# A gated delta rule whose keys keep their length and whose next body's matrices are made inside the solve

## The chip, the cores and the metric
The kernel runs on one core of a Trainium2 chip. The metric is the device time of one execution in microseconds (us), as the median of several runs. TensorE multiplies matrices, VectorE and ScalarE work on elements, GpSimd does the same more slowly and only in SBUF, and SyncE issues the DMAs. PSUM has eight banks of 512 fp32 columns.

## The reference
The program is one decoder layer: a layer norm, a gated delta rule (`L0_attn`), a cross attention, and a feed-forward with block quantisation. The change lies in the delta rule. Of it the reference computes, for 8 sequences of 256 tokens, 8 key heads and 16 value heads of width 128:

```
q, k, v = split(silu(causal_conv(x @ W_qkv)));  z = x @ W_z
q = l2norm(q) * DK**-0.5;  k = l2norm(k)         # x * rsqrt(sum(x*x) + 1e-6)
for t: S = S * exp(g_t);  v_adj = (v_t - k_t S) * beta_t
       S = S + k_t v_adj^T;  o_t = q_t S
o = o * rsqrt(mean(o*o) + 1e-6) * norm_weight * silu(z)
```

## The kernel before, in words
`delta_rule` runs 32 bodies that project and a 33rd that only finishes. A body takes one pair of sequences and one key head with its two value heads. The two sequences are the sets s = 0 and 1, so every buffer of `two(...)` exists twice. Each sequence is cut in two halves of 128 tokens (k = 0, 1); with the two value heads e this makes four blocks hb.

Body n solves the delta rule on q, k and v that body n - 1 projected, and projects q, k, v and z for body n + 1. The projection has six tiles of 128 channels, each of four parts of three matmuls of 512 columns (`project`, L600 to L602), 24 parts in all. The parts are dealt by hand between the steps of the solve. Two PSUM banks `proj` take them in turn. Before, the same two banks also take the decay sums, the outputs turned to channels, the sums of squares and the spread norms.

The solve goes so. `scores` makes key-key products (L622, L623) and key-query products (L628, L629). VectorE masks the key products (L1016), multiplies them by the decay and by beta to the matrix A (L1022), adds the identity to its diagonal half blocks in fp16 (L1029) and makes the first inverse (L1033). TensorE turns it (`first_inverse`, L649). Six levels then double the size of the inverted blocks: `level_r` (L665, or L661 at the last level), a mask by VectorE (L1059), `level_x` (L685 and L690, or L679), and copies by ScalarE to `inv` (L883) and `inv_t` (L887). With the inverse, each half of the tokens is solved once (`solve`, L701), its residual is taken with I + A (`residual`, L712, L1080) and a correction is added (`correct`, L719, L1086). `outputs` (L733) multiplies by the attention matrix, and `between` (L725, L726) carries the first half to the second: L1112 subtracts it from the second values, ScalarE copies them (L920) and scales the other product to `o_off` (L923). The second half is solved in the same way.

Before, keys are scaled to length one: q and k are squared (L914), `sums_of_squares` adds them (L741), VectorE adds epsilon (L1107), GpSimd takes the power -0.5 (L1195) and makes two diagonals (L1199, L1204), TensorE spreads them over the partitions (`spread_norms`, L748), and VectorE multiplies (`k_unit`, L1122). The query's norm is applied to the outputs: `next_gate` makes `q_scale` (L1008, L1011) and copies the gates (L1006).

The short convolution is three taps per tile on VectorE (`tap`, L957) behind two copies by ScalarE (`tile_copy`, L826 and L829). GpSimd also multiplies the mask by the decays (`mask_gates`, L1177), adds the identity to A (L1184), normalises the outputs (L1162 to L1170) and makes two of the steps of silu(z) (L1207, L1189). `gated` (L996) multiplies the outputs by it, and SyncE stores them (`store`, L560). Each fourth body splits the weights of the next key head into a high part (ScalarE, L838) and a low part (VectorE, L971), from tiles that SyncE loads (L555).

Each engine works through its own queue strictly as it is written in `step` of its block. What holds an instruction is a semaphore (`wait_ge`), and everything behind it on the engine waits too.

## Time and profile before

| | |
|---|---|
| median of 3 runs | 2535.69 us (2531.49 to 2535.79) |
| the profiled execution | 2537.05 us |
| its span, first to last instruction | 2535.3 us |
| TensorE / VectorE / ScalarE / GpSimd busy in the span | 2138.2 / 1936.7 / 1439.7 / 1190.9 us |
| projection lines L600, L601, L602 | 378.5 / 319.8 / 314.9 us busy, 768 matmuls each |
| taps, L957 | 388.9 us busy, 384 instructions |

"Busy" is the union of an engine's instructions. In a timeline, rows of one line that follow each other are merged (x2, x4), "idle before" is the engine's gap and what ended it, and an instruction's length can hold its wait for a port. Busy TensorE is overlapped work: what the next matmul adds is read from one start to the next.

### The profile page before, as it was taken

The page shows a single profiled execution, that of the slowest core. Times are in us where ns is not written, and L with a number is a line of the kernel's source. Part 1 is how long each engine was busy: PE and PEld are TensorE (multiplying, and loading weights), DVE is VectorE, ACT ScalarE, POOL GpSimd, SP SyncE. Part 2 cuts the span into 40 slices and gives each one's busy share as a digit, 9 for nine tenths or more (in the row PEclk, how much of TensorE's full clock was granted, in tenths as well). Part 3 has the DMA queues.
Part 4 walks back from the last instruction along what each step waited for, and adds up shares of the span by engine and source line. Part 5 has one row for each costly group of instructions (what it writes and reads, how often), then busy time and mean ns, then how long its engine had stood idle before and what let it go on. Part 6 is the DMA issues. An engine that isn't in the chain of part 4 may idle for free. (4 is left out here: it accounts for less than half of the span.)

```text
span 2535.3 us, 56036 instructions
## 1 busy us (share of the span) xinstructions
PE 2138.2 (84%) x19200; PEld 1571.8 (62%) x19224; DVE 1936.7 (76%) x4154; ACT 1439.7 (57%) x3914; POOL 1190.9 (47%) x1003
## 2 busy tenths in 40 slices
PE   4788888898898899889889888856889898864998
PEld 2566766676676677667667666755566666543444
DVE  7778787777778777777877777754788888863897
ACT  2556555656555565565556556544667777652443
POOL 7544445344444544444454445420566666661332
PEclk8899999999999999999999999968999999986999
DMA  2100000000100100100100000006233333213111
GB/s 69 47 8 25 25 8 21 29 8 14 36 8 8 41 8 8 33 17 8 33 17 8 25 17 17 21 18 189 67 91 96 95 95 95 74 42 125 50 55 48
DMA packets 122857, 107.56 MB, mean 42 GB/s; under 512 B 12080, under 2 KB 97072, under 8 KB 122800
## 3 DMA queue, kind: packets, MB, share of 16 engines
q1 hardware_dynamic: 122800, 106.87, 13.6%
q8 instruction: 28, 0.46, 0.1%
q14 instruction: 29, 0.24, 0.0%
HBM read 72.24 MB, written 34.60 MB: 42 GB/s over the span
## 5 line engine op out<-in xcount | busy, mean ns | idle before, releaser
L957 DVE SCALAR_TENSOR_TENSOR qkv<-conv_in,taps,qkv 128x512 f32<-128x512 f32 x384 | 388.9, 1025 | 8.8 <-ACT qkv L829 8.8
L600 PE MATMUL proj<-xn_hi,w_lo 128*128 x768 | 378.5, 493 | 0.1
L601 PE MATMUL proj<-xn_lo,w_hi 128*128 x768 | 319.8, 416 | 0.2 <-issue 0.2
L602 PE MATMUL proj<-xn_hi,w_hi 128*128 x768 | 314.9, 410 | 0.0
L1195 POOL TENSOR_TENSOR r_norm<-sumsq,neg_half 128x8 f32<-128x8 f32 x32 | 67.2, 2101 | 420.4 <-DVE sumsq L1107 420.4
L1059 DVE TENSOR_TENSOR i_less_r<-bank_c,join_mask 128x256 f16<-128x256 f32 x330 | 124.1, 416 | 171.5 <-PE bank_c L665 171.5
L883 ACT ACTIVATE inv<-bank_b 128x256 f16<-128x256 f32 x330 | 112.4, 382 | 187.1 <-PE bank_b L685 187.0
L1162 POOL TENSOR_TENSOR o_pow<-o_var,neg_half 128x4 f32<-128x4 f32 x68 | 89.4, 1331 | 269.6 <-DVE o_var L989 269.6
L1177 POOL TENSOR_TENSOR g_mask<-mask_ge,gates 128x512 fp32r<-128x512 f32 x132 | 191.9, 1481 | 0.3 <-POOLq L506 0.3
L602 PEld LDWEIGHTS proj<-xn_hi,w_hi 128*128 128x128 f32 x768 | 154.3, 201 | 38.3
L600 PEld LDWEIGHTS proj<-xn_hi,w_lo 128*128 128x128 f32 x768 | 153.7, 200 | 27.3 <-issue 0.2
L601 PEld LDWEIGHTS proj<-xn_lo,w_hi 128*128 128x128 f32 x768 | 155.8, 203 | 12.9 <-issue 0.7
L1658 ACT ACTIVATE probs<-ps_s,shift 128x256 f32<-128x256 f32 x256 | 117.7, 474 | 56.0 <-DVE shift L1779 55.1
L2384 POOL TENSOR_TENSOR i_q<-i,i_scale 128x1024 bf16<-128x1024 fp8e4 x32 | 61.1, 1909 | 168.2 <-DVE i L2341 168.2
L1207 POOL TENSOR_TENSOR z_th<-z_th,z_raw 128x1024 f32<-128x1024 f32 x32 | 78.4, 2450 | 126.4 <-ACT z_th L930 126.4
L1525 PE MATMUL ps_s<-k_blocks,q_t 128*128 128x512 f32 x256 | 129.5, 630 | 1.2 <-issue 1.1
L920 ACT ACTIVATE v_r<-v 128x256 fp32r<-128x256 f32 x66 | 27.6, 417 | 181.3 <-DVE v L1112 181.3
L685 PE MATMUL bank_b<-i_less_r,inv_t 64*64 64x64 f16 x2640 | 97.9, 196 | 37.1 <-DVE i_less_r L1059 35.9
L685 PEld LDWEIGHTS bank_b<-i_less_r,inv_t 64*64 64x64 f16 x2640 | 71.4, 108 | 92.0 <-issue 92.0
L1490 PE MATMUL ps_y<-wo_hi,o_lo 128*128 128x512 f32 x256 | 108.3, 423 | 23.8 <-DVE wo_lo L1927 20.9
L649 PE MATMUL bank_b<-ident,inv_t 64*64 64x64 f16 x528 | 22.4, 213 | 123.4 <-issue 81.6
L1665 ACT ACTIVATE probs<-probs,r_sums 128x256 f32<-128x256 f32 x256 | 109.3, 500 | 26.3 <-DVE r_sums L1784 26.3
(289 smaller groups left out, 6305.4 us busy)
## 6 DMA issues: line engine op xcount, KB each, us to landing
out_t<-o_out SPq DMA_DIRECT2D x68, 256.0 KB, 2.0
o_raw<-out_t SPq DMA_DIRECT2D x32, 512.0 KB, 5.5
w_raw<-in_L_attn_W_qkv_dram SPq DMA_DIRECT2D x36, 256.0 KB, 2.9
wq_dram<-wq_q SPq DMA_DIRECT2D x48, 128.0 KB, 2.2
w_raw<-in_L_attn_W_z_dram SPq DMA_DIRECT2D x18, 256.0 KB, 2.7
x_sb<-in_x_dram SPq DMA_DIRECT2D x16, 256.0 KB, 2.8
x_in<-in_x_dram SPq DMA_DIRECT2D x16, 256.0 KB, 5.8
wq_raw<-in_L_ffn_w_gate_dram SPq DMA_DIRECT2D x16, 256.0 KB, 2.6
```

What stands on the lines that cost most here:

```text
L600: pe.matmul(out, w_lo[:, k, cols], sh.xn_hi[:, k, tok], start=(k == 0), stop=False)
L601: pe.matmul(out, w_hi[:, k, cols], sh.xn_lo[:, k, tok], start=False, stop=False)
L602: product = pe.matmul(out, w_hi[:, k, cols], sh.xn_hi[:, k, tok], start=False, stop=(k == KT - 1))
L685: last = pe.matmul(folded(bank_b[s])[rows, hb, :], inv_t[s][rows, hb, :], i_less_r[s][rows, hb, :], start=True, stop=True)
L883: act.activation(inv[s][:, :, :], folded(bank_b[s]), ACT.Copy).then_inc(t_done[s], 1)
L957: dve.scalar_tensor_tensor(out=out, in0=conv_in[:, j, :, k:k + T], scalar=taps[:, j, k:k + 1], in1=out, op0=ALU.mult, op1=ALU.add).then_in ...
L1059: dve.tensor_tensor(i_less_r[s][:, :, :], folded(bank_c[s]), bcast(sh.join_mask[:, l + 1, :], 1, 4), ALU.mult).then_inc(r_done[s], 1)
L1177: pool.tensor_tensor(g_mask[s][:, i, :, :], bcast(sh.mask_ge[:, :], 1, 4), bcast(g_cols, 2, P), ALU.mult).then_inc(mask_done[s], 1)
L1490: pe.matmul(ps_y[:, :], o_lo[e][:, g, :], wo_hi[:, k, :], start=begin, stop=False)
L1525: last = pe.matmul(ps_s[u][i][:, :], q_t[u][:, c, :], k_blocks[:, c, 2 * i:2 * i + 2, :], start=True, stop=True)
L1658: last = act.activation(probs[u][:, j, :], ps_s[u][j // 2][:, T * (j % 2):T * (j % 2) + T], ACT.Exp, bias=shift[u][:, j:j + 1], scale=SCAL ...
L1665: last = act.activation(probs[u][:, j, :], probs[u][:, j, :], ACT.Copy, scale=r_sums[u][:, j:j + 1])
```

## The change
The change replaces `scores`, `spread_norms`, `keep_scale` and `next_gate`, and deals the steps of all five queues anew.

- Keys are used as they are. The key products are made from raw keys; beta is divided by the key's squared length (`key_gate`: epsilon, reciprocal, product with the gates), the values are multiplied by the key's length (`k_len`, a power 0.5 on GpSimd) when ScalarE copies them (`value_copies`), and the factor that carries the first half is divided likewise (`off_gate`). The query's length goes into the epsilon of the output norm (`q_eps`).
- GpSimd no longer makes diagonals nor the two steps of silu(z); one VectorE instruction (`z_gate`) makes silu(z) at the sixth level.
- Body n makes the decay sums, the decays, the key products, A, I + A and the turned first inverse of body n + 1: the decay sums at the sixth level, the key products behind the first solve, A for set 0 ahead of the update of the second values, A for set 1 ahead of the second residual, `first_inverse` at the end.
- `proj` serves the projection alone. Decay sums, values and turned outputs go to `bank_b`, sums of squares to a free corner of `bank_a`, both output products to `bank_c`.
- `inv` and `inv_t` lie side by side, and so do the products they come from, in one bank: at the first four levels one ScalarE copy of 512 columns per set replaces two of 256.
- `w_decayed` and `o_off` get buffers of their own.
- Values are turned at the second level and outputs to channels at the fourth; `gated` moves from the first level to the fifth, and the taps follow from the second level on.

```diff
+def key_scores(n, made):
+    if made is not None:
+        pe.wait_ge(silu_done, made)
+    for s in S:
+        b0, b1, both = blocks(s)
+        k = qkv[:, 1, :]
+        pe.matmul(bank_a[s][:, 0:2, :], k[:, b0], k[:, both], start=True, stop=True)
+        pe.matmul(bank_a[s][:, 2, :], k[:, b1], k[:, b1], start=True, stop=True).then_inc(kk_ps[s], 1)
...
-    scores(n)
-    parts(0, 5)
-    first_inverse(n)
...
+    query_scores(n)
+    parts(0, 4)
+    level_r(n, 0)
+    parts(4, 5)
+    level_x(n, 0)
+    parts(5, 7)
+    level_r(n, 1)
     values(n)
-    parts(6, 8)
-    for l in range(LEVELS):
-        at, after_r, after_x = ((8, 0, 0), (8, 1, 1), (10, 1, 1), (12, 1, 1), (14, 1, 1), (16, 2, 1))[l]
-        level_r(n, l)
-        if l == 0:
-            to_channels(n, projects)
-        parts(at, at + after_r)
-        level_x(n, l)
-        parts(at + after_r, at + after_r + after_x)
+    level_x(n, 1)
+    parts(7, 8)
+    level_r(n, 2)
+    parts(8, 9)
+    level_x(n, 2)
+    parts(9, 11)
+    level_r(n, 3)
+    to_channels(n, True)
+    level_x(n, 3)
+    parts(11, 12)
+    level_r(n, 4)
+    parts(12, 14)
+    level_x(n, 4)
+    parts(14, 16)
+    level_r(n, 5)
+    if projects:
+        decay_sums(n + 1, n + 1)
+    level_x(n, 5)
+    parts(16, 18)
     for s in S:
         solve(n, 0, s)
-    parts(19, 20)
-    for s in S:
-        residual(n, 0, s)
-    parts(20, 21)
-    for s in S:
-        correct(n, 0, s)
     if projects:
         sums_of_squares(n)
+        key_scores(n + 1, 3 * n + 3)
+    for s in S:
+        residual(n, 0, s, projects)
+    parts(18, 19)
+    for s in S:
+        correct(n, 0, s)
+    parts(19, 20)
     for s in S:
         outputs(n, 0, s)
         between(n, s)
-    parts(21, 23)
+    parts(20, 21)
     for s in S:
         solve(n, 1, s)
+    parts(21, 22)
+    for s in S:
+        residual(n, 1, s, projects)
+    parts(22, 23)
+    for s in S:
+        correct(n, 1, s)
+    parts(23, 24)
+    for s in S:
+        outputs(n, 1, s)
     if projects:
-        spread_norms(n)
-    for s in S:
-        residual(n, 1, s)
-    parts(23, 24)
-    for s in S:
-        correct(n, 1, s)
-    if projects:
-        decay_sums(n + 1)
-    for s in S:
-        outputs(n, 1, s)
-decay_sums(0)
+        first_inverse(n + 1)
+decay_sums(0, None)
+key_scores(0, None)
+first_inverse(0)
...
+def decays(n, used):
+    for s in S:
+        act.wait_ge(d_ps[s], n + 1)
+        if used is not None:
+            act.wait_ge(attn_done[s], used)
+        act.activation(decay[s][:, :, :], bank_b[s][:, :, :], ACT.Exp).then_inc(decay_done[s], 1)
...
+def value_copies(n):
+    act.wait_ge(len_done, n + FIRST)
+    for s in S:
+        act.wait_ge(v_ps[s], n + 1)
+        act.activation(v_r[s][:, :, :], bank_b[s][:, 0:2, :], ACT.Copy, scale=k_len[:, 2 * s:2 * s + 1])
+        act.activation(v[s][:, 0:2, :], bank_b[s][:, 0:2, :], ACT.Copy, scale=k_len[:, 2 * s:2 * s + 1])
+        act.activation(v[s][:, 2:4, :], bank_b[s][:, 2:4, :], ACT.Copy,
+                       scale=k_len[:, 2 * s + 1:2 * s + 2]).then_inc(v_done[s], 1)
...
-                act.activation(inv_t[s][:, :, :], folded(bank_a[s]), ACT.Copy).then_inc(x_done[s], 1)
+                act.activation(inverse[s][:, :, :, :].rearrange("p w h c -> p (w h c)"),
+                               bank_a[s][:, :, :].rearrange("p a c -> p (a c)"),
+                               ACT.Copy).then_inc(t_done[s], 1)
...
+        if l == 0:
+            for s in S:
+                act.wait_ge(a_done[s], n + 1)
+                act.activation(a_low[s][0:H, :, :], a_t[s][0:H, :, H:], ACT.Copy).then_inc(low_done[s], 1)
+        if l == 1:
+            value_copies(n)
         if project:
-            if l in (2, 4):
+            if l in (1, 3):
...
+    if project:
+        decays(n + 1, n + 1)
+        act.wait_ge(silu_done, 3 * n + 3)
+        act.activation(th[:, :, :], qkv[:, 0:2, :], ACT.Square).then_inc(sq_done, 1)
...
+        key_off(n + 1, n + 1)
         tile_copy(n, 5)
-        act.wait_ge(proj_ev, TILES * n + TILES)
+        act.wait_ge(proj_ev, TILES * n + TILES + BANKS)
         act.activation(z_th[:, :, :], z_raw[:, :, :], ACT.Tanh, scale=0.5).then_inc(z_th_done, 1)
-    for s in S:
-        act.wait_ge(o_ps[s], 2 * n + 1)
-        act.activation(o[s][:, 0:2, :], bank_a[s][:, 0:2, :], ACT.Copy).then_inc(o0_done[s], 1)
+        inverse_turned(n + 1)
...
+def z_gate(n):
+    dve.wait_ge(z_th_done, n + FIRST)
+    for s in S:
+        dve.wait_ge(out_done[s], n + 1)
+    dve.scalar_tensor_tensor(out=z_silu[:, :, :], in0=z_th[:, :, :], scalar=1.0, in1=z_raw[:, :, :],
+                             op0=ALU.add, op1=ALU.mult).then_inc(z_done, 1)
...
+def key_gate(n):
+    dve.wait_ge(ss_ps, n + FIRST)
+    dve.tensor_scalar(sumsq[:, :], bank_a[0][:, 3, 0:8], EPS, None, ALU.add).then_inc(ss_done, 1)
+    dve.wait_ge(ss_done, n)
+    dve.reciprocal(k_inv[:, :], sumsq[:, 4:8]).then_inc(inv_done, 1)
+    dve.wait_ge(inv_done, n)
+    dve.tensor_tensor(gate[:, :, :].rearrange("p s (k e) -> p s k e", k=2),
+                      sh.gates[:, bass.ds(2 * n, 2), 0:4].rearrange("p s (k e) -> p s k e", k=2),
+                      bcast(k_inv[:, :].rearrange("p (s k) -> p s k", k=2), 3, 2),
+                      ALU.mult).then_inc(gate_done, 1)
...
+    dve.tensor_copy(gate_off[:, :, 0:2], sh.gates[:, bass.ds(2 * n, 2), 4:6])
+    dve.tensor_tensor(gate_off[:, :, 2:4], sh.gates[:, bass.ds(2 * n, 2), 6:8],
+                      bcast(k_inv[:, :].rearrange("p (s k) -> p s k", k=2)[:, :, 0], 2, 2),
                       ALU.mult).then_inc(gate_done, 1)
...
+    for s in S:
+        dve.wait_ge(ovar[s], n)
+    dve.tensor_copy(q_eps_last[:, :], q_eps[:, :]).then_inc(eps_done, 1)
+    dve.wait_ge(eps_done, 2 * n - 1)
+    dve.tensor_scalar(q_eps[:, :], sumsq[:, 0:4], float(DK) * EPS, None, ALU.mult).then_inc(eps_done, 1)
...
+def matrix(n, s, used):
+    dve.wait_ge(kk_done[s], n + 1)
+    dve.wait_ge(decay_done[s], n + 1)
+    if used is not None:
+        dve.wait_ge(gate_done, 2 * used - 1)
+        dve.wait_ge(ia_done[s], used)
+        dve.wait_ge(low_done[s], used)
...
         if l == 0:
+            variances(n)
+            attention(0)
+        if l == 1:
+            attention(1)
+            taps_of((0, 0))
+        if l == 2:
+            taps_of((1, 0), (0, 1))
+        if l == 3:
+            taps_of((1, 1), (0, 2), (1, 2))
+        if l == 4:
             gated(n)
-        if l == 5:
-            attention(0)
-        if project:
-            if l in (1, 2):
-                tap(n, 1, l - 1)
-                tap(n, 0, l)
-            if l == 3:
-                tap(n, 1, 2)
-            if l == 4:
+            if project:
                 silu(n, 1)
                 silu(n, 2)
-            if next_g is not None and l in (1, 3):
-                split(l // 2, TILES * next_g + l // 2 + 1)
+        if l == 5:
+            z_gate(n)
+            taps_of((2, 0))
+        if next_g is not None and l in (2, 3):
+            split(l - 2, TILES * next_g + l - 1)
...
+    if project:
+        for s in S:
+            key_diagonal(n + 1, s)
     take_residual(0)
-    v_tap(2, 1)
+    taps_of((2, 1))
     if next_g is not None:
         split(2, TILES * next_g + 3)
     for s in S:
         add_correction(0, s)
...
         for e in range(2):
...
     if project:
-        dve.wait_ge(ss_ps, n + 1)
-        dve.tensor_scalar(sumsq[:, :], proj[0][:, 0:8], EPS, None, ALU.add).then_inc(ss_done, 1)
-    v_tap(2, 2)
+        key_gate(n + 1)
+        taps_of((2, 2))
+        matrix(n + 1, 0, n + 1)
     for s in S:
         dve.wait_ge(yz_ps[s], n + 1)
         for e in range(2):
...
-    v_tap(3, 0)
+    taps_of((3, 0))
     if next_g is not None:
         split(3, TILES * next_g + 4)
     if project:
...
-        dve.tensor_tensor(k_unit[:, :], qkv[:, 1, :], proj[0][:, :], ALU.mult).then_inc(k_done, 1)
+        matrix(n + 1, 1, n + 1)
     take_residual(1)
-    v_tap(3, 1)
+    taps_of((3, 1))
     for s in S:
         add_correction(1, s)
-    v_tap(3, 2)
+    taps_of((3, 2))
     if project:
-        next_gate(n + 1)
+        off_gate(n + 1)
...
+def with_identity(n, used):
+    for s in S:
+        pool.wait_ge(a_done[s], n + 1)
+        if used is not None:
+            pool.wait_ge(aw_ps[s], used)
+        pool.tensor_tensor(ia_t[s][:, :, :], a_t[s][:, :, :], bcast(sh.ident[:, :], 1, 4),
+                           ALU.add).then_inc(ia_done[s], 1)
 def step(n, project):
     normalise(n)
-    for s in S:
-        pool.wait_ge(a_done[s], n + 1)
-        pool.tensor_tensor(ia_t[s][:, :, :], a_t[s][:, :, :], bcast(sh.ident[:, :], 1, 4),
-                           ALU.add).then_inc(ia_done[s], 1)
-    pool.wait_ge(z_mul, n + FIRST)
-    for s in S:
-        pool.wait_ge(out_done[s], n + 1)
-    pool.tensor_tensor(z_silu[:, :, :], z_th[:, :, :], z_raw[:, :, :], ALU.add).then_inc(z_done, 1)
     if project:
         for s in S:
             pool.wait_ge(d_ps[s], n + 1)
         mask_gates(n + 1)
         pool.wait_ge(ss_done, n + 1)
-        pool.tensor_tensor(r_norm[:, :], sumsq[:, :], sh.neg_half[:, :], ALU.pow).then_inc(rn_done, 1)
...
-        pool.wait_ge(z_th_done, n + 1)
-        pool.tensor_tensor(z_th[:, :, :], z_th[:, :, :], z_raw[:, :, :], ALU.mult).then_inc(z_mul, 1)
+        for s in S:
+            pool.wait_ge(v_done[s], n + 1)
+        pool.tensor_tensor(k_len[:, :], sumsq[:, 4:8], pos_half[:, :], ALU.pow).then_inc(len_done, 1)
+        with_identity(n + 1, 2 * n + 2)
```

## Rows read from the trace of the kernel before

**Rows 1.** Four bodies in stretches: stretch, us, busy of each engine, PEclk, DMA, GB/s.
```profile
717.00:764.86 47.86, 42.69 (x456) 33.63 (x455) 37.03 (x84) 28.43 (x83) 23.02 (x20) 0.96 0.03 11
...
812.72:864.36 51.64, 44.19 (x456) 34.54 (x455) 40.84 (x88) 30.51 (x88) 23.57 (x20) 0.93 0.10 30
...
864.36:913.57 49.21, 42.38 (x455) 33.58 (x455) 38.30 (x88) 29.14 (x84) 22.82 (x20) 0.97 0.07 21
...
1652.64:1704.13 51.49, 31.48 (x362) 26.93 (x361) 26.88 (x74) 24.35 (x88) 15.20 (x16) 0.64 0.03 11
```

**Rows 2.** Timeline of TensorE, one body: start, us, engine, line, what, [idle before].
```profile
726.63 0.64 PE L649 MATMUL bank_b<-ident,inv_t 64*64 64x64 f16 x16 [3.27 <-issue]
...
752.90 0.56 PE L719 MATMUL bank_c<-v_r,inv_r 128*128 128x128 f32 x4
...
755.05 0.69 PE L733 MATMUL bank_a<-w,attn_t 128*128 128x128 f32 x4
...
757.56 0.58 PE L600 MATMUL proj<-xn_hi,w_lo 128*128 x1
...
759.15 0.56 PE L701 MATMUL bank_c<-v_r,inv_r 128*128 128x128 f32 x4
...
759.55 0.45 PE L748 MATMUL proj<-diag,ones_r 128*128 128x512 f32 x1
...
760.63 0.50 PE L748 MATMUL proj<-diag,ones_r 128*128 128x512 f32 x1 [0.63 <-POOL diag L1204]
...
760.97 1.05 PE L712 MATMUL bank_b<-w,ia_t 128*128 128x128 f32 x8
...
762.95 0.45 PE L612 MATMUL proj<-g_mask,mask_lt_r 128*128 128x512 f32 x1
...
763.98 1.05 PE L733 MATMUL bank_c<-w,attn_t 128*128 128x128 f32 x8
```

**Rows 3.** Timeline of VectorE in the same body.
```profile
716.85 2.28 DVE L1008 TENSOR_SCALAR q_scale<-r_norm 128x4 f32<-128x4 f32 x1
...
720.41 1.14 DVE L1022 SCALAR_TENSOR_TENSOR a_t<-decay,gate,kk_diag 128x128 f32<-128x128 f32 x4
...
722.48 0.29 DVE L1033 TENSOR_TENSOR inv_t<-a_half,join_mask 128x256 f16<-128x256 f16 x1
...
727.96 0.75 DVE L957 SCALAR_TENSOR_TENSOR qkv<-conv_in,taps,qkv 128x512 f32<-128x512 f32 x1 [0.28 <-ACT qkv L829]
...
735.77 3.50 DVE L957 SCALAR_TENSOR_TENSOR qkv<-conv_in,taps,qkv 128x512 f32<-128x512 f32 x2
...
753.39 0.41 DVE L1086 TENSOR_TENSOR w<-w,bank_c 128x256 f32<-128x256 f32 x1
...
755.22 0.17 DVE L1107 TENSOR_SCALAR sumsq<-proj 128x8 f32<-128x8 f32 x1
...
756.64 0.61 DVE L1112 SCALAR_TENSOR_TENSOR v<-bank_b,gate,v 128x128 f32<-128x128 f32 x2 [0.57 <-PE bank_b L726]
...
761.87 0.75 DVE L1080 TENSOR_TENSOR v_r<-v,bank_b 128x256 fp32r<-128x256 f32 x2
```

**Rows 4.** Timeline of GpSimd in the same body.
```profile
716.66 2.44 POOL L1207 TENSOR_TENSOR z_th<-z_th,z_raw 128x1024 f32<-128x1024 f32 x1 [3.95 <-ACT z_th L930]
...
725.90 2.65 POOL L1162 TENSOR_TENSOR o_pow<-o_var,neg_half 128x4 f32<-128x4 f32 x2 [6.80 <-DVE o_var L989]
...
730.88 2.50 POOL L1184 TENSOR_TENSOR ia_t<-a_t,ident 128x512 f32<-128x512 f32 x2
...
737.24 5.83 POOL L1177 TENSOR_TENSOR g_mask<-mask_ge,gates 128x512 fp32r<-128x512 f32 x4
```

**Rows 5.** Timeline of ScalarE in the same body.
```profile
728.99 0.59 ACT L873 ACTIVATE v<-bank_a 128x512 f32<-128x512 f32 x1
...
751.07 1.06 ACT L914 ACTIVATE th<-qkv 128x1024 f32<-128x1024 f32 x1
...
758.92 1.13 ACT L923 ACTIVATE qk_diag<-bank_b,gate 128x128 f32<-128x128 f32 x4
```

More of the change, by code:

```diff
@@ L447, in delta_rule @@
         g_mask = [sb(f"g_mask{s}", [P, 2, 4, P], F32R) for s in S]
-        inv_t = [sb(f"inv_t{s}", [P, 4, H], F16) for s in S]
-        inv = [sb(f"inv{s}", [P, 4, H], F16) for s in S]
+        inverse = [sb(f"inverse{s}", [P, 2, 4, H], F16) for s in S]
+        inv, inv_t = ([inverse[s][:, which, :, :] for s in S] for which in range(2))
         i_less_r = [sb(f"i_less_r{s}", [P, 4, H], F16) for s in S]
@@ L527, in _ @@
                 pool.memset(z_silu[:, :, :], 0.0)
-                pool.memset(k_unit[:, :], 0.0)
-                pool.memset(r_norm[:, :], 0.0)
+                pool.memset(k_len[:, :], 1.0)
+                pool.memset(pos_half[:, :], 0.5)
                 for s in S:
@@ L540, in _ @@
                     dve.memset(z[:, :, :], 0.0)
-                dve.memset(q_scale[:, :, :], 0.0)
-                for done in (conv, k_done, *o1_done, *res_done):
+                dve.memset(gate[:, :, :], 0.0)
+                dve.memset(gate_off[:, :, :], 0.0)
+                dve.memset(q_eps[:, :], 1.0)
+                dve.memset(q_eps_last[:, :], 1.0)
+                for done in (conv, z_done, *o1_done, *res_done):
                     dve.sem_inc(done, FIRST)
@@ new lines, in matrix @@
+                def matrix(n, s, used):
[5 more added lines that the diff above has]
+                        dve.wait_ge(low_done[s], used)
+                    for hb in range(4):
+                        last = dve.scalar_tensor_tensor(out=a_t[s][:, hb, :], in0=decay[s][:, hb, :],
+                                                        scalar=gate[:, s, hb:hb + 1], in1=kk_diag[s][:, hb // 2, :],
+                                                        op0=ALU.mult, op1=ALU.mult)
+                    last.then_inc(a_done[s], 1)
+                    dve.wait_ge(a_done[s], n + 1)
+                    for rows in HALVES:
+                        last = dve.tensor_tensor(a_half[s][rows, :, :], a_t[s][rows, :, rows],
+                                                 bcast(sh.ident[rows, rows], 1, 4), ALU.add)
+                    last.then_inc(half_done[s], 1)
+                    dve.wait_ge(half_done[s], n + 1)
+                    dve.tensor_tensor(inv_t[s], a_half[s][:, :, :], bcast(sh.join_mask[:, 0, :], 1, 4),
+                                      ALU.mult).then_inc(x0_done[s], 1)
```

325 lines of the change are left out of this document (127 added, 198 removed).

## The prediction
> **What bounds the kernel now.** I read the page first: one core, 56036 instructions, TensorE busy 2138 of 2535 us, VectorE 1937, and the three projection lines L600 to L602 alone 1013 us. They belong to the delta rule, 33 bodies from about 79 to 1704 us; the change touches nothing else. So I then took single bodies [rows 1]. An ordinary one lasts 47.86 us with TensorE busy 42.69, VectorE 37.03, ScalarE 28.43 and GpSimd 23.02. Each fourth body prepares the next weights and lasts 51.64, and the one behind it is longer too. The last, without projection, lasts 51.49 to the final transposes.
>
> The remaining 5.17 us of an ordinary body are waits of TensorE. The timeline [rows 2] shows 3.27 us before the first transposes of the inverse and 0.64 us in the spreading of the norms; 1.26 us are spread over the levels. The granted clock is 0.96 [rows 1]: 3.8 us of the body run at 1.2 GHz, behind the 3.27 us wait. Up to 1.9 us are lost by it; part falls on short work, and I take 1.3.
>
> What ends the 3.27 us is on VectorE [rows 3]. q_scale, four elements wide, takes 2.28 us from 716.85; GpSimd's product z_th runs from 716.66 for 2.44 us [rows 4], and q_scale ends with it. Behind it in VectorE's order stand the last outputs, both key diagonals and both matrices (L1022 to L1033, 2.36 us each), for which the transposes wait.
>
> The Trainium skill, "SBUF — State Buffer", section "Who interferes with whom", says that VectorE and GpSimd share a port pair under an exclusive lock, which some single-input VectorE modes and VectorE instructions with two SBUF inputs take. The q_scale row agrees.
>
> **What goes.** (a) The 3.27 us wait and its 1.3 us of slow clock: the matrices are now made in the body before. (b) The spreading of the norms, 759.55 to 760.97 [rows 2], 1.42 us with its wait, 0.8 without. (c) GpSimd loses both z products, two diagonals and the splitting of the norms; its mask products and its sums with the identity stay. (d) q_scale goes. (e) k_unit goes; scalars take its place. All other matmuls keep their number and size. TensorE's own work at full clock is therefore 42.69 - 0.8 - 1.3 = 40.6 us per body, the floor.
>
> **What comes: the tail, from the first correction (call its start c).** The body before shows its work [rows 2]: outputs and both products between the halves 755.05 to 757.56, 2.5 us; a solve 759.15 to 759.55, 0.4; residual, one part and correction 760.97 to 762.95, 2.0; last outputs 763.98 to 764.86, 0.9; a first correction 0.4; transposes 0.6 by the busy time of the L649 row; four more parts at 0.8 (two took 757.56 to 759.15). Together 10.0 us. The rest, 30.6 us, is the head.
>
> VectorE cannot follow this tail. In the trace c is 752.90; the first sum of corrections starts at 753.39 and the decayed values end where sumsq begins, 755.22 [rows 3], so c+2.3. New order behind that:
> - sumsq, reciprocal, gate product: three small ones at 0.2, c+2.9; tap (2,2) 0.7, c+3.6.
> - matrix of set 0, 2.36 us: c+6.0. It stands ahead of the update of the second values, which before came at once.
> - that update, 0.55 per set: c+6.5 and c+7.1. ScalarE's copy of 256 columns 0.4 (512 take 0.59 [rows 5]): the second solve can start at c+7.0. TensorE is there at c+0.4+0.8+2.5+0.8 = c+4.5. Wait **2.5 us**.
> - ScalarE copies set 1 by c+7.6, makes o_off (1.1 us [rows 5]) and copies w: residuals end at c+10.0 instead of 9.5. Wait **0.5**.
> - VectorE: tap to c+7.8, matrix of set 1 with a_half to c+9.9. Here GpSimd's identity sums, 1.25 us each [rows 4], are released by these same residuals and read SBUF, so they meet a_half or inv_t. Taps against GpSimd's work took 3.50 us for two instead of 1.4 [rows 3]: the blocking is 1 us each. I take 1.1 for inv_t: c+11.2, residual 0.8 (L1080): c+12.0, tap under the second sum c+12.9, correction sums c+13.6. Bounds: 0 (no overlap) and 2.5 (both sums in full).
> - TensorE waits **1.2** for the second correction and **0.4** for the last outputs; then outputs, transposes: c+14.6.
>
> Tail 14.6, of which 4.6 wait.
>
> **The head** has four meetings; ScalarE first. Tile copies and value copies now sit between the second and third copy of the inverse: six copies of at most 0.6, about 1.8, and a tile copy of two at 0.59. Two parts plus level, about 3.5 us of TensorE's work, nearly cover them. VectorE's taps behind them meet the mask products (5.83 us for four [rows 4]): 0.4 at the third level and 0.2 at the fourth. The three taps before the fifth cost 0.5 and the longer copies 0.1. The square of q and k (1.06 [rows 5]) stands behind the new exponentials (two at 0.59): its sums come 0.8 late. Total **2.0 us**, with bounds 0.8 (only the square) and 4 (each once more). Joining two inverse copies into one of 512 columns: a ScalarE copy of that size takes 0.59 [rows 5] and ends about 0.2 later than before for set 0; one part of projection covers it. Value 0, bounds -0.5 and +0.6. silu(z) as one VectorE instruction costs 1.2 us there, hidden: VectorE then idles over 3 us until the key scores.
>
> **The clock.** The 2.5 us wait may cost it again. Rows show the fall behind 3.27 us. A fall would hit mostly the tail, where TensorE waits for VectorE anyway. I take 0.4, bounds 0 and 1.3.
>
> Body: 40.6 + 2.0 + 4.6 + 0.4 = 47.6, against 47.86: 0.26 less, times 32 = **-8 us**. In a group of four with weights the fourth body and its follower are 3.8 and 1.35 us over an ordinary one [rows 1]. Splits 4 and 5 (0.7 each) stood before the matrices on the waiting chain and now stand before work with a slack of one microsecond; two others move into the tail. The output stores leave SyncE some ten microseconds later, at the fifth level, and the loads of weight tiles 3 to 5 stand behind them in its queue; tile 3 is first used after the first solve, ten microseconds on, so this costs nothing unless a load takes longer than that. I take 1.5 off per group, eight groups: **-12** (bounds 0 and -24). Ends: the last body had TensorE at 31.48 busy of 51.49 and its matrices are now ready, -11; the first has to make its matrices before its projections, +5: **-6** (bounds -12 and +3).
>
> Sum -26 us. The profiled execution took 2537.05 us around its span of 2535.3; against it the time is 2511, 25 under the median 2535.69 of the runs. Predicted: **2511 us**.
>
> **Rivals.**
> A, the forecast (chance 0.35): old wait and norm spreading traded for tail waits; 2511, own range 2490 to 2530.
>
> B, the tail is nearly free (0.27): matrix 1 and identity sums don't meet (-1.1) and the clock holds (-0.4), head waits stay under 1.2 (-0.8): 45.3 us per body, 2511 - 2.3x32 = 2437. For it: the released instructions are close in time and VectorE may win each time. Against: GpSimd waits for just these residuals and has nothing else to do. Half of it gives 2474.
>
> C, slower (0.25): the second solve. VectorE reaches c later than TensorE because key diagonals, residual and tap (2,1) follow the key scores at once; matrix 0 then ends past c+7, the wait exceeds the 3.27 us that cost the clock before, and the slow stretch runs on into the projections of the next head. Price: 0.8 wait, 0.9 clock, 0.4 taps, 2.1 us per body: 2511 + 67 = 2578. It decides once VectorE is 0.8 us later than laid out at the matrix; below that it is case A. For: VectorE has no gap there in my layout. Against: it idles before the key scores.
>
> D, the lock on the power (0.08): k_len's power is released by sumsq together with reciprocal and gate product, which read SBUF. In the trace a tap at 727.96 takes its 0.75 us while powers run from 725.90 for 2.65 [rows 3, 4], so a power doesn't hold VectorE for its length. The Trainium skill, same page and section, says that whoever comes first holds the pair for the whole instruction. By that rule the gate product would wait the length of a power. That is 1.0 us (half of 2.65 less 0.3) on the tail's chain: 2511 + 32 = 2543. The trace speaks against it.
>
> E, nothing is gained (0.05): same within 5 us: the released work is refilled by waits exactly, 2536.
>
> **How the numbers follow.** A measurement tells 0.2%, 5 us. Faster: B whole (0.27), most of A (0.29 of 0.35), 0.04 of the rest: 0.60. Same: 0.03 of A, E, a little of C and D: 0.10. Slower: 0.30. Range: from 2450, leaving the lower end of B out, to 2570, leaving the worst of C out.
>
> **What would show it.** The wait before the transposes L649 gone, no instruction in place of q_scale with over 1 us; a wait of 2 to 3 us before the second solve, ended by v_r from ScalarE; waits of 1 us before the second correction; inv_t or a_half of set 1 stretched while GpSimd adds the identity; granted clock between 0.96 and 1. Bodies near 47.6 us. It is wrong if the second solve doesn't wait (then B), if the clock's slow stretch stays and falls on projections (C), or if level waits exceed 4 us.

## The result, and the profile after

The changed kernel takes 2652.66 us (median of 4 runs, 2648.56 to 2654.09) against 2535.74 of the kernel before beside it (4 runs, 2531.49 to 2541.91): ratio 1.0456, 95% interval 1.0432 to 1.0481, 117 us slower. The forecast was 2511, with a range of 2450 to 2570. The profiled span grew from 2535.3 to 2646.8 us.

From the page of the kernel after: busy time of each engine (share, instructions), the granted clock of TensorE in 40 slices (in tenths of 2.4 GHz; 9 stands for 90% or more), and three groups of instructions.

```profile
PE 2226.2 (84%) x19160; PEld 1631.8 (62%) x19160; DVE 1925.6 (73%) x4150; ACT 1446.2 (55%) x3716; POOL 834.4 (32%) x742
...
PEclk8788899898899899899988889986999999987999
...
L977 DVE SCALAR_TENSOR_TENSOR qkv<-conv_in,taps,qkv 128x512 f32<-128x512 f32 x384 | 309.7, 827 | 0.0
...
L671 PE MATMUL bank_a<-i_less_r,inverse 64*64 64x64 f16 x2640 | 98.5, 199 | 91.7 <-DVE i_less_r L1100 91.4
...
L1083 DVE SCALAR_TENSOR_TENSOR attn_t<-decay,gate,qk_diag 128x128 f32<-128x128 f32 x264 | 172.0, 710 | 0.0
```

GpSimd fell from 1190.9 to 834.4 us, VectorE's taps from 388.9 to 309.7, and TensorE has 64 weight loads fewer (40 matmuls in the records, of which a few can be missing); still TensorE is busy 88 us longer. In the slices of the delta rule, which nearly all stood at 9 before, 8 and 9 now mix, and the mean clock of the whole run fell from 0.935 to 0.906: TensorE ran longer at 1.2 GHz, the lower of its two levels.

The windows of bodies, from one L615 to the next, as in [rows 1] from one L622 to the next: two ordinary ones, one that prepares weights, its follower, and the last.

```profile
773.29:824.87 51.58, 44.62 (x452) 34.47 (x453) 37.20 (x85) 28.59 (x77) 11.87 (x11) 0.93 0.03 10
824.87:876.51 51.64, 45.59 (x452) 35.95 (x453) 36.30 (x85) 28.17 (x76) 12.34 (x11) 0.90 0.03 10
876.51:933.38 56.87, 47.73 (x453) 37.59 (x453) 40.23 (x88) 31.61 (x84) 12.01 (x11) 0.88 0.09 28
933.38:984.71 51.33, 44.63 (x452) 34.54 (x453) 38.22 (x87) 29.07 (x78) 11.75 (x11) 0.93 0.06 20
1775.96:1818.24 42.28, 27.02 (x337) 22.43 (x337) 20.48 (x52) 22.35 (x77) 7.15 (x8) 0.73 0.04 14
```

An ordinary body has grown from 47.86 to 51.58 us, by 3.72: TensorE is idle 6.96 instead of 5.17 us and busy 44.62 instead of 42.69, with fewer matmuls. A clock of 0.93 between its two levels means about 7 us of the body at half speed. What they cost is read further down, against the same work at full clock.

Over all 32 bodies that project (87.02 to 1775.96, before 77.64 to 1652.64) the growth is 113.9 us: TensorE's idle time rose from 194.9 to 221.9 us and its busy time from 1380.1 to 1467.1. With no work added, three quarters of the loss are TensorE working more slowly, not waiting.

TensorE's own waits from 100 to 1600 us, some 29 bodies: total, times, longest.

```profile
PE bank_a L671 <- DVE i_less_r L1100: 80.3, 29, 2.9
PE bank_c L688 <- ACT v_r L938: 64.5, 28, 2.4
PE bank_a L727 <- ACT th L919: 18.9, 29, 1.1
PE bank_c L707 <- DVE v_r L1126: 18.7, 15, 2.2
```

Every body now waits at L671, 2.8 us in the mean, the update of the inverse. The timeline of TensorE in the body from 773.29 shows where:

```profile
788.18 0.31 PE L671 MATMUL bank_a<-i_less_r,inverse 64*64 64x64 f16 x8 [2.80 <-DVE i_less_r L1100]
...
788.88 0.79 PE L585 MATMUL proj<-xn_hi,w_lo 128*128 x1
...
790.32 0.63 PE L585 MATMUL proj<-xn_hi,w_lo 128*128 x1
...
803.77 1.95 PE L727 MATMUL bank_a<-ones,th 128*128 128x1 f32 x16 [0.53 <-ACT th L919]
...
810.21 0.56 PE L707 MATMUL bank_c<-v_r,inv_r 128*128 128x128 f32 x4
...
817.19 0.93 PE L688 MATMUL bank_c<-v_r,inv_r 128*128 128x128 f32 x4 [2.35 <-ACT v_r L938]
...
821.53 0.77 PE L707 MATMUL bank_c<-v_r,inv_r 128*128 128x128 f32 x4 [0.74 <-DVE v_r L1126]
...
823.21 1.16 PE L720 MATMUL bank_c<-w,attn_t 128*128 128x128 f32 x8 [0.16 <-DVE w L1132]
```

The first row is the third level. Behind it the projection's matmuls take 0.63 us each, against 0.40 in the same body elsewhere. The windows of those stretches (the clock is the third number from the end) give two falls, both in the head, ahead of the first correction at 810.21 (what lies behind it is the tail):

```profile
785.30:788.84 3.54, 0.74 (x33) 0.69 (x32) 3.54 (x5) 2.16 (x6) 1.85 (x2) 1.00 0.00 0
788.84:792.25 3.41, 3.41 (x29) 2.32 (x22) 0.90 (x3) 0.90 (x2) 0.00 (x0) 0.50 0.00 0
805.90:809.32 3.42, 3.42 (x15) 3.14 (x14) 1.10 (x3) 0.00 (x0) 0.00 (x0) 0.50 0.00 0
```

In the first, TensorE was busy 0.74 of the 3.54 us ahead of it and then worked without a gap for 3.41 us at half clock. The second begins in the key scores, behind the 0.53 us wait and the sixteen one-column matmuls L727.

The next body, at 824.87, has a third fall, in its tail, behind the wait at the second solve:

```profile
870.75:874.16 3.41, 3.41 (x15) 3.12 (x15) 2.41 (x7) 0.32 (x2) 2.54 (x2) 0.50 0.00 0
```

It is busy 0.97 us longer than the body at 773.29 and idle 0.91 us less, and its length is the same within 0.1 us: in the tail TensorE waits for VectorE anyway, so a slow stretch there costs next to nothing. The two in the head stand on work that was ready.

What makes the third level late is read on VectorE and GpSimd:

```profile
778.76 1.13 DVE L1083 SCALAR_TENSOR_TENSOR attn_t<-decay,gate,qk_diag 128x128 f32<-128x128 f32 x4
...
782.09 4.16 DVE L1083 SCALAR_TENSOR_TENSOR attn_t<-decay,gate,qk_diag 128x128 f32<-128x128 f32 x4
...
786.17 1.52 DVE L977 SCALAR_TENSOR_TENSOR qkv<-conv_in,taps,qkv 128x512 f32<-128x512 f32 x1
...
787.62 0.74 DVE L1100 TENSOR_TENSOR i_less_r<-bank_c,join_mask 128x256 f16<-128x256 f32 x2
```
```profile
778.85 2.11 POOL L1209 TENSOR_TENSOR o_scale<-o_var,neg_half 128x4 f32<-128x4 f32 x2 [8.15 <-DVE o_var L998]
...
780.93 2.04 POOL L1212 TENSOR_TENSOR o<-o,o_scale 128x512 f32<-128x512 f32 x2
...
782.92 4.22 POOL L1219 TENSOR_TENSOR g_mask<-mask_ge,gates 128x512 fp32r<-128x512 f32 x4
```

The attention products L1083 (decay x gate x query scores) of set 0, four instructions, take 1.13 us; the same four of set 1 take 4.16. They run while GpSimd streams 512 columns, the end of the output product (L1212) and then the mask products (L1219). The power before them (o_scale) ran beside the attention of set 0 and did not stretch it. Behind the 4.16 us stand a tap and the mask instruction L1100, for which L671 waits.

### The profile page after: what moved, and what is told of

It reads as the page before. It is cut to its first block and busy times, and to the rows that moved or that the text cites. A ratio compares the mean times of both kernels' runs of the same rounds, so it can differ in the third digit from the quotient of the medians.

```text
span 2646.8 us, 55594 instructions
## 1 busy us (share of the span) xinstructions
PE 2226.2 (84%) x19160; PEld 1631.8 (62%) x19160; DVE 1925.6 (73%) x4150; ACT 1446.2 (55%) x3716; POOL 834.4 (32%) x742
## 5 line engine op out<-in xcount | busy, mean ns | idle before, releaser
L977 DVE SCALAR_TENSOR_TENSOR qkv<-conv_in,taps,qkv 128x512 f32<-128x512 f32 x384 | 309.7, 827 | 0.0
L1240 POOL TENSOR_TENSOR k_len<-sumsq,pos_half 128x4 f32<-128x4 f32 x32 | 32.2, 1006 | 831.7 <-DVE sumsq L1023 831.7
L890 ACT ACTIVATE inverse<-bank_a 128x512 f16<-128x512 f32 x264 | 143.2, 595 | 233.7 <-PE bank_a L675 233.7
L1100 DVE TENSOR_TENSOR i_less_r<-bank_c,join_mask 128x256 f16<-128x256 f32 x330 | 124.4, 417 | 174.8 <-PE bank_c L654 174.7
L828 ACT ACTIVATE z_raw<-proj 128x512 f32<-128x512 f32 x64 | 38.2, 597 | 345.2 <-PE proj L587 345.2
L671 PE MATMUL bank_a<-i_less_r,inverse 64*64 64x64 f16 x2640 | 98.5, 199 | 91.7 <-DVE i_less_r L1100 91.4
L1083 DVE SCALAR_TENSOR_TENSOR attn_t<-decay,gate,qk_diag 128x128 f32<-128x128 f32 x264 | 172.0, 710 | 0.0
L1209 POOL TENSOR_TENSOR o_scale<-o_var,neg_half 128x4 f32<-128x4 f32 x68 | 71.0, 1055 | 304.9 <-DVE o_var L998 304.8
L671 PEld LDWEIGHTS bank_a<-i_less_r,inverse 64*64 64x64 f16 x2640 | 72.0, 111 | 140.0 <-issue 139.8
L1228 POOL TENSOR_TENSOR ia_t<-a_t,ident 128x512 f32<-128x512 f32 x66 | 92.1, 1415 | 209.2 <-PE bank_b L700 202.2
L1219 POOL TENSOR_TENSOR g_mask<-mask_ge,gates 128x512 fp32r<-128x512 f32 x132 | 140.6, 1092 | 0.3 <-POOLq L490 0.3
L1525 PE MATMUL ps_y<-wo_hi,o_lo 128*128 128x512 f32 x256 | 108.1, 422 | 21.6 <-DVE wo_lo L1962 18.7
```

The costliest lines, as they stand in the source:

```text
L671: pe.matmul(folded(bank_a[s])[rows, hb, :], inv_t[s][rows, hb, :], i_less_r[s][rows, hb, :], start=True, stop=True)
L890: act.activation(inverse[s][:, :, :, :].rearrange("p w h c -> p (w h c)"), bank_a[s][:, :, :].rearrange("p a c -> p (a c)"), ACT.Copy).the ...
L977: dve.scalar_tensor_tensor(out=out, in0=conv_in[:, j, :, k:k + T], scalar=taps[:, j, k:k + 1], in1=out, op0=ALU.mult, op1=ALU.add).then_in ...
L1083: last = dve.scalar_tensor_tensor(out=attn_t[s][:, hb, :], in0=decay[s][:, hb, :], scalar=gate[:, s, hb:hb + 1], in1=qk_diag[s][:, hb // 2 ...
L1100: dve.tensor_tensor(i_less_r[s][:, :, :], folded(bank_c[s]), bcast(sh.join_mask[:, l + 1, :], 1, 4), ALU.mult).then_inc(r_done[s], 1)
L1219: pool.tensor_tensor(g_mask[s][:, i, :, :], bcast(sh.mask_ge[:, :], 1, 4), bcast(g_cols, 2, P), ALU.mult).then_inc(mask_done[s], 1)
```

## The experiments

Each ratio is against runs of the kernel before on the same chip, with its 95% interval. The theory under test: GpSimd's streams hold the attention of set 1, the wait at the third level puts the clock down, and the half clock falls on projections.

**1. The attention of set 1 moved up one level**, next to that of set 0 and ahead of GpSimd's products.

```
 if l == 0:
     variances(n)
     attention(0)
-if l == 1:
     attention(1)
+if l == 1:
     taps_of((0, 0))
```

> The changed kernel with both attention products made at the first level (set 1 was made at the second). Theory 1 (port and clock): at the second level GpSimd's output product and mask product block VectorE's four attention instructions (4.16 us instead of 1.13), TensorE waits 2.8 us before the third level_x and its clock then stands at half for 3.4 us of projections. Then the four instructions take about 1.1 us again, the 2.8 us wait and that slow stretch go, an ordinary body falls from 51.6 to 47.5 to 48.5 us, the run to 2520 to 2560. Theory 2 (tail): the loss lies in the wait of 2.35 us before the second solve, behind the matrix of set 0; then this edit moves less than 1 us per body, 2620 to 2655.

Measured: 2517.93 us, ratio 0.9922 [0.9896, 0.9949], 135 us below the changed kernel. One row of its VectorE timeline, and three of its waits from 100 to 1600 us:

```profile
732.59 2.18 DVE L1083 SCALAR_TENSOR_TENSOR attn_t<-decay,gate,qk_diag 128x128 f32<-128x128 f32 x8
```
```profile
PE bank_c L688 <- ACT v_r L938: 71.9, 31, 2.4
...
PE bank_c L707 <- DVE v_r L1126: 12.5, 11, 2.2
...
PE bank_a L671 <- DVE i_less_r L1100: 0.8, 1, 0.8
```

All eight take 2.18 us, the wait at L671 is gone (0.8 us once in 31 bodies), and the wait at the second solve, up to 2.4 us, has stayed. So another place for four small instructions is enough to undo the whole regression. Over the 32 bodies TensorE's idle time falls by 76 us and its busy time by 60: so what goes is the wait and, only a little less, the slow clock behind it. Ordinary bodies are near 48 us, the size that the prediction had.

**2. GpSimd waits instead**: its output product starts only when the attention of set 1 is done (`behind` is true in every body); nothing else is changed.

```
 for s in S:
     pool.wait_ge(opow[s], n + 1)
+    if behind:
+        pool.wait_ge(attn_done[1], n + 1)
     pool.tensor_tensor(o[s], ...)
```

> The changed kernel; the one edit is a wait: GpSimd starts its output product, and the mask products behind it, only when VectorE has made the attention of set 1. VectorE's order and all work are unchanged; it only takes GpSimd off the port while those four instructions run. If GpSimd's use of the shared port makes them last 4.16 us, they take about 1.1 us, TensorE's 2.8 us wait before the third level_x goes and the time falls near that of a_attn: 2510 to 2565. If they are slow for another reason (their operands, ScalarE's copies beside them), they stay at 4 us and the time at 2645 or above, since a wait was added.

Measured: 2547.63 us, ratio 1.0043 [1.0025, 1.0061], 105 us below the changed kernel. One body of it:

```profile
737.71 1.13 DVE L1083 SCALAR_TENSOR_TENSOR attn_t<-decay,gate,qk_diag 128x128 f32<-128x128 f32 x4
```
```profile
738.92 2.48 POOL L1214 TENSOR_TENSOR o<-o,o_scale 128x512 f32<-128x512 f32 x2 [2.35 <-DVE attn_t L1083]
```

At its old place the attention takes 1.13 us once GpSimd stands still. That separates the two readings of experiment 1 (order on VectorE, or GpSimd's streams): with VectorE's order unchanged, holding GpSimd back brings 105 of the 135 us. The taps behind still meet its products (two take 2.46 us at 742.93, and three behind the products 2.18), and L671 waits 21.8 us in 31 bodies.

**3. Filling the wait.** In front of the third level TensorE does eight 512-column matmuls whose result nobody uses, in the changed kernel as it was.

```
 parts(8, 9)
+for _ in range(8):
+    pe.matmul(bank_a[1][:, :, :], sh.ones_r[:, :], sh.xn_hi[:, 0, 0:N2], start=True, stop=True)
 level_x(n, 2)
```

> The changed kernel with eight matmuls of 512 columns without use (1.9 us of work at full clock) put ahead of the third level_x, where TensorE waits 2.8 us. It prices the clock by itself. If the fall of the clock behind that wait costs time, the added work removes the slow stretch and the run gets faster by 1.2 to 1.5 us per body: 2600 to 2615. If the clock costs nothing because other engines are late anyway, the time stays within 5 us of 2652, or grows where the fillers outlast the wait.

Measured: 2569.39 us, ratio 1.0110 [1.0068, 1.0152], 83 us below the changed kernel, with work added.

```profile
759.92 2.00 PE L761 MATMUL bank_a<-xn_hi,ones_r 128*128 128x512 f32 x8
...
762.89 0.31 PE L671 MATMUL bank_a<-i_less_r,inverse 64*64 64x64 f16 x8 [0.98 <-DVE i_less_r L1102]
```

What VectorE has to do ahead of its mask instruction is unchanged; only TensorE's idle time is less. The attention of set 1 still takes 4.16 us (756.80), and the eight matmuls fill the wait that they stand in. From the start of this body to 779.89, well past the third level, the clock is now full:

```profile
748.00:779.89 31.89, 30.30 (x372) 23.33 (x373) 21.04 (x39) 23.16 (x62) 8.31 (x8) 1.00 0.04 16
```

So over half of the 135 us of experiment 1 comes back with VectorE as late as it was. 83 us over 32 bodies are 2.6 us each, more than one slow stretch costs and more than I expected. The traces say where the rest is: over the 32 bodies busy time rose by only 6 us although the added matmuls are some 60, so about 50 us less are lost to the clock; idle time fell by 78 us, of which the filling takes 58 and the wait at the second correction (L707, 18.7 us in 29 bodies before, 4.1 in 30 now) some 16. Why that second wait shrinks was not isolated.

**4. The sums of squares.** A part of the projection is put ahead of them (part 18), so that ScalarE's square is done when they come.

```
+parts(18, 19)
 sums_of_squares(n)
 ...
 for s in S:
     residual(n, 0, s, projects)
-parts(18, 19)
```

> The changed kernel with the 19th projection part moved ahead of the sums of squares, so that it covers the 0.53 us wait for the squares. Theory 1 expects 0.5 us per body, and, if the second slow stretch (805.9 to 809.3 in the trace) comes from that wait with the one-column matmuls behind it, up to 1.5 us more: 2590 to 2640. Theory 2 expects nothing: the part is only moved from one place with slack to another, 2645 to 2655.

Measured: 2605.66 us, ratio 1.0267 [1.0230, 1.0303], 47 us lower; the wait at L727 falls from about 19 to 2.1 us in the same stretch. That is 1.5 us per body for a wait of 0.6, so here too something beyond the wait is gained: over the 32 bodies 27 us are idle time and 20 busy time. With experiment 1 it is worth less:

> The changed kernel with two edits, both attention products at the first level and the 19th part ahead of the sums of squares. It splits the 105 us between a_attn (2518) and a_comb (2413). If the part is worth by itself what it was alone (47 us), 2465 to 2480, and the taps have the rest. If the parts of the gain multiply through the clock, it is nearer one of the two ends.

Measured: 2485.96 us, ratio 0.9805 [0.9764, 0.9847], 32 us under experiment 1, a little above the expected 2465 to 2480.

**5. The second values updated before the matrix of set 0**, in the changed kernel. The second solve then has its input early, and the matrix ends late.

```
-    matrix(n + 1, 0, n + 1)
 for s in S:
     (update of the second values)
+if project:
+    matrix(n + 1, 0, n + 1)
```

> The changed kernel with the update of the second values ahead of the matrix of set 0 on VectorE, nothing else. Theory 2 (the tail's order is the loss): the wait before the second solve (2.35 us) goes and 1.5 to 2.3 us per body with it: 2580 to 2605. Theory 1 (VectorE's chain as a whole is too long for the tail): the wait goes there, but both matrices now stand ahead of the second residual, the wait before the second correction grows from 0.7 to about 3 us, and the time stays at 2640 to 2670; the longer single wait may cost a stretch of slow clock.

Measured: 2718.54 us, ratio 1.0740 [1.0683, 1.0796], 66 us above the changed kernel and above both expected ranges.

```profile
PE bank_c L707 <- DVE v_r L1126: 109.4, 27, 4.6
PE bank_a L671 <- DVE i_less_r L1100: 77.8, 28, 2.8
...
PE bank_c L688 <- ACT v_r L938: 2.8, 17, 0.2
```

The 2.35 us wait is gone from L688 and one of 4 us stands at L707: two waits have become one, and a longer one, for their sum per body rises from 2.9 to 4.2 us. Over the 32 bodies 33 us of the loss are idle time and 33 busy time. 24 idle matmuls of 256 columns ahead of that correction:

> The kernel a_v2 (2719 us) with 24 matmuls of 256 columns without use (about 2.9 us of work at full clock) ahead of the second correction, where TensorE waits 3.9 us. If a_v2 lost its 66 us because one long wait costs the clock where two short ones did not, the fillers give 1.5 to 2.5 us per body back: 2635 to 2670. If it lost them by VectorE's order, they give nothing: 2715 to 2725.

Measured: 2659.64 us, ratio 1.0492 [1.0463, 1.0521], 59 us lower with work added, inside the expected range. The windows of 700 to 1500 us, experiment 5 first and then with the idle matmuls, show the clock (third number from the end):

```profile
700.00:1500.00 800.00, 684.01 (x6608) 536.52 (x6606) 565.63 (x1223) 430.06 (x1121) 176.50 (x159) 0.87 0.05 18
```
```profile
700.00:1500.00 800.00, 720.41 (x7152) 571.68 (x7151) 581.91 (x1276) 441.78 (x1167) 184.37 (x165) 0.92 0.05 17
```

**6. All mends together**: experiments 1 and 4, and three taps moved into the gap of 4.79 us in which VectorE waits for the key scores.

```
+taps_of((2, 1), (2, 2), (3, 0))
 if project:
     for s in S:
         key_diagonal(n + 1, s)
 take_residual(0)
-taps_of((2, 1))
 ...
-taps_of((2, 2))
 ...
-taps_of((3, 0))
```

> The changed kernel with three edits: both attention products at the first level, the 19th part ahead of the sums of squares, and the taps (2,1), (2,2) and (3,0) in VectorE's 4.8 us of idling before the key diagonals instead of in the tail. Theory 1: on top of the 2518 of the first edit, 0.5 us per body from the part, 1.4 us from the taps where VectorE's chain ends the waits, and a slow stretch less in some bodies: ordinary bodies of 45.5 to 46.5 us, 2440 to 2480. If the tail is bound by something else than VectorE's chain, 2500 to 2518.

Measured: 2412.58 us, ratio 0.9511 [0.9489, 0.9532], better than expected, and the fastest kernel together with the next. Two ordinary bodies (windows) and the two largest waits of the delta rule:

```profile
673.00:717.02 44.02, 41.56 (x452) 32.12 (x453) 33.80 (x84) 28.67 (x78) 12.62 (x11) 1.00 0.03 12
717.02:762.06 45.04, 42.63 (x453) 33.72 (x453) 33.79 (x85) 28.11 (x77) 12.63 (x11) 0.96 0.03 12
```
```profile
PE bank_c L688 <- ACT v_r L938: 48.4, 31, 1.9
PE bank_c L654 <- ACT inverse L890: 22.8, 71, 1.0
```

The first has full clock throughout and is the cleanest reading of TensorE's own work: 41.56 us, with 2.46 idle. The second has the same waits (2.41 idle) and one slow stretch, 755.23 to 758.64, and takes 1.0 us longer; so this is what one such stretch costs here, less than the 1.7 us that half of its length would be. It stands in the tail too, but the combination has no wait left behind it that could hide it. Two more taps and the key gate in the same gap:

> The kernel a_comb (2413 us) with the taps (3,1) and (3,2) and the key gate (sumsq, reciprocal, product) also moved from VectorE's tail to the idling around the key diagonals. VectorE's chain ahead of the second solve is 0.5 us shorter, and TensorE's wait there (1.5 us) falls by as much: 10 to 25 us, 2388 to 2403. If the longer series of taps makes the key diagonals or the first residual late, 2410 to 2430.

Measured: 2411.76 us, ratio 0.9506 [0.9479, 0.9533], the same time, where the main case expected 2388 to 2403: L688 waits 26.6 instead of 48.4 us in the same stretch, but L707, which waited 0.8, now waits 39.1.

The order of experiment 5 on top of the combination:

> As the last one, with the update of the second values ahead of the matrix of set 0. VectorE's chain has the same length, so both theories expect the sum of the tail's waits unchanged; it stands in one place (the second correction) instead of two. If the clock depends on how long one wait is, this is slower than the last one by 1 to 1.5 us per body where that wait is over 2 us, otherwise equal within 10 us.

Measured: 2513.45 us, ratio 0.9907 [0.9883, 0.9930], 101 us slower than the combination. L688 waits 11.5 us instead of 48.4, L707 105.4, up to 3.8 at a time, and two bodies show:

```profile
720.28:767.63 47.35, 42.98 (x452) 33.55 (x453) 35.45 (x83) 28.44 (x77) 12.45 (x11) 0.96 0.03 11
767.63:814.65 47.02, 42.72 (x452) 33.31 (x453) 35.43 (x83) 28.40 (x77) 12.46 (x11) 0.97 0.03 11
```

In these two TensorE is busy about as long as in the combination's body of 45.04 us; its idle time is 4.3 instead of 2.4 us. But they are not typical: over the 32 bodies idle time rises by 64 us and busy time by 46. So here too the loss is the wait and, for four tenths of it, the clock.

**7. The old wait alone**, in the kernel before: what is q_scale's 2.28 us worth without the rest of the change? Its two instructions moved behind the matrices.

```
+def next_scale(n):
+    dve.wait_ge(gate_done, 4 * n + 2)
     (the two instructions of q_scale)
 ...
 (both matrices)
+next_scale(n)
```

> The kernel before, with the two q_scale instructions moved behind the two matrices (they were at the body's end, where GpSimd's z product blocks the first for 2.28 us instead of 0.17). If that block is what makes TensorE wait 3.27 us before the transposes of the inverse, the wait falls to about 1.0 us, the slow clock behind it goes, and a body loses 2.3 to 3.6 us: 2420 to 2465. If the wait has another cause, for instance the copies of ScalarE, the time stays near 2536.

Measured: 2512.73 us, ratio 0.9908 [0.9874, 0.9942], a gain of 24 us where 71 to 116 were expected. The block moved on: the copy of the gates (L1006) took its place in a third of the bodies (0.17 us at the least, 2.35 at most, 0.94 in the mean), and TensorE still waits there (100 to 1600 us):

```profile
PE bank_b L649 <- issue: 58.0, 24, 3.3
PE bank_b L649 <- ACT qk_off L863: 33.2, 7, 5.0
```

With the gates also ahead of the last tap:

> The kernel before, with q_scale behind the matrices as in b_late and next_gate ahead of the last tap. In b_late the copy of the gates took the block in a third of the bodies (0.94 us in the mean instead of 0.17). If GpSimd's product holds the port, a copy issued 0.7 us earlier comes ahead of it, no instruction is blocked there, and all ordinary bodies last the 45.4 us that some of b_late's do: 2460 to 2495. If the copy is late for another reason, 2513 as b_late.

Measured: 2488.92 us, ratio 0.9816 [0.9794, 0.9837]. The copy and q_scale now take 0.17 us each, and 2.1 us of the wait stay (50.3 us, 24 times): the key diagonals and both matrices stand between the key scores and the transposes. So the block was worth 1.2 of the 3.3 us of wait, and both moves together 47 us.

**Where the time went.** TensorE over the 32 bodies that project, from the windows of each trace (start of the first body to start of the 33rd), in us. From the changed kernel on the work is the same in all rows but the two with idle matmuls, so between the others a change in busy time is, but for small differences in how matmuls overlap, the clock.

| kernel | length | busy | idle |
|---|---|---|---|
| before | 1575.0 | 1380.1 | 194.9 |
| changed | 1688.9 | 1467.1 | 221.9 |
| 1, attention moved | 1553.3 | 1407.5 | 145.7 |
| 2, GpSimd waits | 1583.1 | 1418.5 | 164.6 |
| 3, wait filled | 1616.8 | 1473.4 | 143.5 |
| 4, part ahead | 1641.9 | 1447.5 | 194.4 |
| 5, second values first | 1755.6 | 1500.5 | 255.1 |
| 5, filled | 1699.0 | 1531.0 | 168.0 |
| 6, combination | 1446.5 | 1355.7 | 90.7 |
| 6, with the order of 5 | 1556.8 | 1402.1 | 154.8 |

## Why the prediction was wrong

Two steps failed. The wait at the third level was put at 0.4 us and measured 2.80, because the attention of set 1, blocked beside GpSimd, was costed nowhere. The term of the clock was put at 0.4 us and measured 3.0, because that wait stands ahead of projections in the head and not in the tail.

The clock's price is read by comparing the head and the tail of the body at 773.29 with those of a body of the combination that has full clock throughout and the same TensorE work. Heads first, then tails; the changed kernel stands first in each pair:

```profile
773.29:810.21 36.92, 33.51 (x378) 25.99 (x378) 23.02 (x44) 22.84 (x61) 8.30 (x8) 0.91 0.04 14
...
673.00:704.13 31.13, 30.50 (x377) 23.44 (x377) 21.91 (x46) 23.05 (x62) 8.62 (x8) 1.00 0.05 17
```
```profile
810.21:824.87 14.66, 11.11 (x76) 8.48 (x75) 14.19 (x42) 5.75 (x16) 3.57 (x3) 1.00 0.00 0
...
704.13:717.02 12.89, 11.06 (x75) 8.68 (x76) 11.89 (x39) 5.62 (x16) 3.99 (x3) 1.00 0.00 0
```

By the prediction's own steps:

- **Right, what goes, (a) to (e)**: the wait before the transposes, q_scale, the spreading and k_unit are gone. **The floor was 1.0 us too low**: 40.6 forecast, 41.56 measured at full clock. The head's 30.6 was met (30.50); the tail's own work measured 11.1 and not 10.0.
- **Right in length, the tail, and partly by luck.** With the first correction c at 810.21 the second solve starts at c+6.98 (forecast c+7.0, TensorE there at c+4.6 instead of c+4.5) and the body ends at c+14.66 (forecast c+14.6). Its waits were 2.35, 0.74 and 0.16 instead of 2.5, 1.2 and 0.4, the residual's 0.5 didn't come. So the waits were 1.1 us below the forecast 4.6 (3.55 idle in all) and the work 1.1 above the forecast 10.0, and the two errors cancel. inv_t of set 1 took 1.40 us instead of 0.29 beside GpSimd's sum with the identity (819.72, 2.56 us): 1.1, as laid out.
- **Right, the case against rival D**: GpSimd's power runs 812.65 to 813.66, and the gate product at 812.95, inside it, takes 0.17 us. The rule that D took up did not hold for a power of four elements.
- **Wrong, the head.** Forecast 33.0 us to c (30.6, 2.0 of waits, 0.4 of clock), measured 36.92. All of the miss in a body is here: 1.4 of it waits, 2.6 clock. The waits sum to 3.4 instead of 2.0: the third level waits **2.80 instead of 0.4**, the squares 0.53 instead of 0.8, the fourth and fifth level not at all. The step "VectorE's taps behind them meet the mask products: 0.4 at the third level" looked at the taps alone. The attention of set 1, which stands right ahead of them, was costed nowhere; and in the changed kernel GpSimd's mask products follow its output product at once (780.93, 782.92), since the identity sums and the z product that lay between them have moved or gone.
- **Wrong, and larger: the clock.** "I take 0.4, bounds 0 and 1.3", with the ground that a fall would hit mostly the tail. Two stretches of 3.4 us at half clock lie in the head of this body, on work that TensorE had ready; they cost 3.0 us (33.51 busy against 30.50). The ground was right where it applied, as the third fall shows, but it did not ask what a wait in the head would do. The total idle time of a body, 6.96 us, is near the forecast 6.6; I had laid out one long wait, 2.5 us in the tail, and short ones, and a second long one of 2.8 came in the head. The term of 0.4 measured 3.0, and its upper bound of 1.3 was below the price of one such stretch in the head (1.5). Experiments 1 to 3 show the chain: without the blocked attention 135 us go, without GpSimd beside it 105, with the wait filled by idle matmuls 83.
- **Wrong, the weight groups** (-12): fourth body and follower are 5.3 and -0.3 us over an ordinary one, 5.0 together, against 3.8 and 1.35 [rows 1]. 0.1 was saved instead of 1.5.
- **The ends** (-6): the first L615 starts at 87.02, the first L622 before at 77.64: 9.4 later, not 5. The last body takes 42.28 instead of 51.49: -9.2, near the forecast -11. Together nothing. The 32 bodies between grew by 113.9 us, and the span by 111.5.

Rival C had the sign but not the cause: VectorE started matrix 0 at c+3.5, as laid out, and the second solve's wait stayed under 3.27. Its last clause, the slow clock on the head's projections, came true by another wait. Its price of 2.1 us per body was too low: 3.6 were lost.

**Open.** What starts the second slow stretch was not isolated: experiment 4 took away the 0.53 us wait and moved the one-column matmuls behind a part of projection in one step. And in the combination ordinary bodies of 44.0 and 45.0 us have the same idle time; the second have one slow stretch and the first none, and what decides which body gets it is open. So is which of the prediction's readings of the tail left out 1.1 us of TensorE's work.

## What to carry to other kernels

When work is taken off GpSimd, look at what its remaining long streams now fall on: here every VectorE instruction with two SBUF inputs that ran beside one had to be costed, however small, and was best put at a time when GpSimd stands still. Cost a wait of TensorE by its length and by what stands behind it: here a wait of 2.8 us ahead of ready work cost itself and about 1.5 us of slow clock, and a slow stretch with a further wait behind it cost next to nothing. Idle matmuls in a wait are a cheap test of how much of its price is the clock. And read the price of a slow stretch over all bodies: one or two bodies can show it or hide it.
